# Start, output and routing table of a four-stage transformer kernel: first batch taken alone, output rows written by the last five tiles, last product in halves, table of tiles on GpSimd

## The reference

```python
x = x + xattn0(layernorm(x), ctx, Wq, Wkv, Wout)          # 16 heads of 16, softmax
x = x + ffn0(layernorm(x), ...)                           # 704 hidden, fake-quantised to 8 bits, silu(gate) * up
x = x + xattn1(layernorm(x), ctx, ctx, gates...)          # 4 heads of 64, mLSTM decay, RMS norm
x = x + ffn1(layernorm(x), gate_w, w1, w3, w2)            # 8 experts of 1024, the best 2 of each token
# ffn1: probs = softmax(x @ gate_w); top 2, weights normalised to sum 1;
#       sum over the two experts of weight * ((silu(x @ w1) * (x @ w3)) @ w2)
```

## Time and profile before

| what | value |
|---|---|
| time, median of 3 runs | 757.08 us (752.0 to 757.09) |
| time of the profiled execution | 756.54 us |
| its span | 754.8 us |
| busy: TensorE, VectorE, ScalarE, GpSimd | 657.7, 500.0, 375.3, 291.9 us |
| chain that ended last, by engine | TensorE 58%, VectorE 20%, issue 8%, ScalarE 5%, DMA 2% |
| mean granted clock of TensorE | 0.952 of 2.4 GHz |

### The profile page before, as it was taken

The page is one execution under the profiler, slowest core; times in us unless marked ns, Lnnn a source line. Parts: engine busy times, 40 slices in busy tenths (PEclk is TensorE's granted clock), DMA queues, the critical chain, the costliest instruction groups (busy, mean ns, idle before and its releaser), DMA issues.

```text
span 754.8 us, 17035 instructions
## 1 busy us (share of the span) xinstructions
PE 657.7 (87%) x4890; PEld 464.8 (62%) x4890; DVE 500.0 (66%) x1180; ACT 375.3 (50%) x878; POOL 291.9 (39%) x358
## 2 busy tenths in 40 slices
PE   2799999997777776898099999999999999999992
PEld 2588888886534545786056666666666666666661
DVE  6389899998588967797954746555464747554430
ACT  1366666665686643786223535363543635543320
POOL 3111111121153625577233736464553637543321
PEclk9799999999999999699589999999999999999996
DMA  8200000000300005336405253533415264421114
GB/s 282 47 15 14 14 14 14 14 0 1 112 0 1 0 1 172 128 82 226 135 23 174 49 150 76 150 85 84 140 31 153 73 181 126 116 43 29 31 15 125
DMA packets 47414, 59.01 MB, mean 78 GB/s; under 512 B 13328, under 2 KB 41168, under 8 KB 47056
## 3 DMA queue, kind: packets, MB, share of 16 engines
q1 hardware_dynamic: 39808, 47.72, 19.5%
q0 software_dynamic: 7536, 10.44, 7.8%
HBM read 145.96 MB, written 11.73 MB: 209 GB/s over the span
## 4 chain that ended last, share of the span: by engine, by line
PE 58%; DVE 20%; issue 8%; ACT 5%; DMA 2%; POOL 2%; DVEq 2%; ACTq 1%; SPq 0%; POOLq 0%
PE psum L1052 19%; PE psum L1074 11%; PE psum L752 5%; PE psum L1065 4%; PE psum L736 3%; PE psum L759 3%; PE psum L772 2%; ACT region L1346 2%; PE psum L791 1%; PE psum L741 1%; PE psum L714 1%; DVE region L1759 1%; DVE region L1777 1%; PE psum L779 1%; DVE region L1956 1%
## 5 line engine op out<-in xcount | busy, mean ns | idle before, releaser
L1052 PE MATMUL psum<-region 128*128 (+1 forms) x936 | 214.8, 379 | 1.6 <-DVE region L1952 1.6
L1052 PEld LDWEIGHTS psum<-region 128*128 128x128 bf16 x936 | 91.5, 98 | 95.5 <-DVE region L1952 1.2
L1329 ACT ACTIVATE region<-psum 128x512 f32<-128x512 f32 x78 | 46.5, 597 | 179.6 <-PE psum L1052 178.7
L675 POOL DMA_INDIRECT sum_dram<-region,row_token x39 | 75.2, 1927 | 135.3 <-DVE region L1948 135.3
L1074 PE MATMUL psum<-region 128*128 (+1 forms) x936 | 110.5, 275 | 5.3 <-DVE region L1956 5.3
L1074 PEld LDWEIGHTS psum<-region 128*128 128x128 bf16 x936 | 91.4, 99 | 18.9 <-issue 7.5
L1931 DVE TENSOR_TENSOR region<-psum,region 128x512 f32<-128x512 f32 x78 | 53.8, 690 | 68.3 <-ACT region L1329 68.3
L545 POOL TENSOR_TENSOR region<-region,pair_mask 128x256 f32<-128x256 f32 x32 | 21.3, 687 | 128.3 <-ACT region L1114 128.3
L1956 DVE TENSOR_TENSOR region<-psum,region 128x1024 bf16<-128x1024 f32 x39 | 47.6, 1221 | 17.7 <-ACT region L1337 17.5
L667 POOL DMA_INDIRECT region<-xrow_dram,row_token x39 | 41.4, 1062 | 38.0 <-DVE row_token L1917 13.6
L1421 DVE TENSOR_REDUCE region<-psum 128x8 f32<-128x1024 f32 x32 | 39.0, 1218 | 18.4 <-PE psum L752 18.4
(11 more groups left out here) (298 smaller groups left out, 1220.3 us busy)
## 6 DMA issues: line engine op xcount, KB each, us to landing
region<-in_L_ffn_w SPq DMA_DIRECT2D x117, 1024.0 KB
region<-in_ctx SPq DMA_DIRECT2D x32, 128.0 KB, 2.4
xrow_dram<-region SPq DMA_DIRECT2D x1, 2080.0 KB, 7.8
x_sb<-in_x SPq DMA_DIRECT2D x4, 512.0 KB, 8.0
region<-in_ctx SPq DMA_DIRECT2D x2, 1024.0 KB, 7.0
region<-neg_max_dram SPq DMA_DIRECT2D x1, 2048.0 KB, 11.5
sum_dram<-x_sb SPq DMA_DIRECT2D x1, 2048.0 KB, 7.5
region<-neg_max_dram SPq DMA_DIRECT2D x4, 256.0 KB, 4.0
```

The lines of the kernel that those rows point to most:

```text
L675: pool.indirect_dma_start(sum_dram, bass.IndirectOffsetOnAxis(ap=row_token[:, t:t + 1], axis=0), y_d[:, t % 2, :], None, compute_op=ALU.ad ...
L1052: last = mm(psum[:, 2 * f + n, :], (xT_lo if xl else xT_hi)[:, p, k, :], weights_at(place, wl, n, k * F1 + f * FH, FH), start=(i == 0), st ...
L1329: act_fn(sil_d[:, f, :], psum[:, 2 * f, :], ACT.Silu).then_inc(sil_d_ready, 1)
```

## The change

1. **Start.** SyncE loads batch 0 of x alone, then context 0, Wq, Wkv, batches 1 to 3, context 1, batches 4 to 7, Wout, batches 8 to 15. VectorE makes the statistics of batch 0, norms it, goes on with batches 1 to 3, norms batch 1, then batches 4 to 7; batches 8 to 11 and 12 to 15 are made inside steps 0 and 1. GpSimd's powers are in five lots (`X_LOTS`), the last three behind the masks of batches 0, 1 and 3. The products wait for Wq and Wkv only. TensorE gets 14, 2 and 6 fillers ahead of the transposes, the products and the scores of batch 0.
2. **Table of tiles.** The lines 1858 to 1874 leave VectorE. GpSimd computes the same table in 27 instructions, from `eend`, ahead of its first gather. VectorE waits for `info_ready` 2, which GpSimd gives behind that gather, ahead of its first low half of the weights, and takes x's low part ahead of the second. TensorE's 40 fillers become 20.
3. **Weight loads.** SyncE's loop over the tiles is written out, and each tile's expert and flag are read once instead of three times.
4. **Output.** After 34 of the 39 additions (`DIRECT`) SyncE copies `sum_dram` to the output. For each of the last five tiles GpSimd gathers the sums of its rows (`gather_sums`, the first from `sum_dram`, the others from the output), VectorE adds them to the weighted product, and GpSimd writes the rows to the output (`write_rows`). The gather waits until the write of the tile before has landed, the writes wait for SyncE's copy.
5. **Last product.** The 16 matmuls with the high part of h of the last tile come first, behind five fillers, without a wait for the low part; the 8 with the low part follow.

```diff
@@ start, SyncE
-            sp.dma_start(x_sb[:, 0:4, :], x_v[:, 0:4, :]).then_inc(x_loaded[0], 16)
+            sp.dma_start(x_sb[:, 0:1, :], x_v[:, 0:1, :]).then_inc(x_loaded[0], 16)
+            sp.dma_start(ctx_sb[:, 0, :], ctx_in[0, :, :]).then_inc(ctx_loaded[0], 16)
             sp.dma_start(wq_sb[:], wq.rearrange("(t p) n -> p t n", p=P)).then_inc(w_loaded, 16)
-            sp.dma_start(ctx_sb[:, 0, :], ctx_in[0, :, :]).then_inc(ctx_loaded[0], 16)
             sp.dma_start(wkv_sb[:], wkv.rearrange("(t p) n -> p t n", p=P)).then_inc(w_loaded, 16)
+            sp.dma_start(x_sb[:, 1:4, :], x_v[:, 1:4, :]).then_inc(x_loaded[1], 16)
...
@@ start, GpSimd
+            X_LOTS = (slice(0, 1), slice(1, 4), slice(4, 8), slice(8, 12), slice(12, B))
+            def x_rstd(i):
+                part = X_LOTS[i]
+                pool.wait_ge(ln_chain, 3 * part.stop)
+                nc.gpsimd.tensor_tensor(rstd[:, part], rstd[:, part], minus_half[:, part], ALU.pow).then_inc(rstd1_ready, 1)
...
             for b in range(B):
                 mask_k(b, b % 2)
+                if b in X_RSTD_AT:
+                    x_rstd(X_RSTD_AT.index(b) + 2)
@@ start, TensorE
+            keep_clock(START_CLOCK[0], 7)
             front_transposes(0, 0, 1)
-            pe.wait_ge(w_loaded, 48)
+            keep_clock(START_CLOCK[1], 7)
+            pe.wait_ge(w_loaded, 32)
             front_products(0, 0)
+            keep_clock(START_CLOCK[2], 7)
             step(0, 0, loads=1)
@@ start, VectorE
+            x_stats(0, 1)
+            norm(0, 0)
+            x_stats(1, 4)
+            norm(1, 1)
+            x_stats(4, 8)
...
-            step(0, 0)
+            step(0, 0, late=[lambda: x_stats(8, 12)])
             late = [[] for b in range(B)]
+            late[1] = [lambda: x_stats(12, B)]
@@ table, GpSimd
+            pool.wait_ge(d_chain, ENDS_STEP)
+            for e in range(E):
+                nc.gpsimd.tensor_scalar(ended[:, 0, e, :], iota_t, eend[:, e:e + 1], None, ALU.is_ge)
+            link_p(nc.gpsimd.tensor_scalar(eend2, etiles, 0.5, None, ALU.is_gt))
+            link_p(tt(ended[:, 1, :, :], ended[:, 0, :, :], eend2.unsqueeze(2).to_broadcast([P, E, NT]), ALU.mult))
+            link_p(tt(ended[:, :, 0:4, :], ended[:, :, 0:4, :], ended[:, :, 4:8, :], ALU.add))
+            link_p(tt(ended[:, :, 0:2, :], ended[:, :, 0:2, :], ended[:, :, 2:4, :], ALU.add))
...
+            nc.gpsimd.tensor_scalar(te, te, -1.0, float(E), ALU.mult, ALU.add).then_inc(info_ready, 1)
+
+            pool.wait_ge(chosen_ready, 3)
             pool.wait_ge(rows_stored, 64)
             gather_rows(0)
+            nc.gpsimd.memset(pause_p[:, 0:1], 0.0).then_inc(info_ready, 1)
@@ table, VectorE
-            link_d(tt(tcmp, eend.unsqueeze(1).to_broadcast([P, NT, E]), iota_t.unsqueeze(2).to_broadcast([P, NT, E]), ALU.is_le))
-            link_d(nc.vector.tensor_reduce(te, tcmp, AX.X, ALU.add))
...
+            dve.wait_ge(info_ready, 2)
             first_low(0)
-            first_low(1)
-            info = [None, tile_values(1)]
...
             x_low(0, 0)
+            first_low(1)
+            info = [None, tile_values(1)]
             first_low(2)
@@ output, GpSimd
+            def gather_sums(t):
+                pool.wait_ge(sum_added, 16 * t)
+                pool.wait_ge(y_ready, t)
+                rows = bass.IndirectOffsetOnAxis(ap=row_token[:, t:t + 1], axis=0)
+                if t == DIRECT:
+                    pool.indirect_dma_start(sums_sb[:], None, sum_dram, rows).then_inc(gather_begun, 16)
+                else:
+                    pool.indirect_dma_start(sums_sb[:], None, out_rows, rows, bounds_check=B * P - 1, oob_is_err=False).then_inc(gather_begun, 16)
+            def write_rows(t):
+                pool.wait_ge(y_ready, t + 1)
+                pool.wait_ge(out_stored, 16)
+                pool.indirect_dma_start(out_rows, bass.IndirectOffsetOnAxis(ap=row_token[:, t:t + 1], axis=0),
+                                        y_d[:, t % 2, :], None, bounds_check=B * P - 1, oob_is_err=False).then_inc(sum_added, 16)
...
-            for t in range(NT - 3, NT):
-                add_rows(t)
+            for t in range(NT - 3, NT):
+                write_rows(t)
+                if t + 1 < NT:
+                    gather_sums(t + 1)
@@ output, SyncE and VectorE
+            sp.wait_ge(sum_added, 16 * DIRECT)
+            sp.dma_start(out_rows, sum_dram[0:B * P, :]).then_inc(out_stored, 16)
+            sp.wait_ge(out_stored, 16)
             sp.wait_ge(sum_added, 16 * NT)
-            sp.dma_start(out.rearrange("b p d -> (b p) d"), sum_dram[0:B * P, :]).then_inc(out_stored, 16)
...
+                    dve.wait_ge(gather_begun, 16 * (t - DIRECT) + 32)
+                    nc.vector.scalar_tensor_tensor(out=y_d[:, p, :], in0=psum[:, 7, 0:D], scalar=w_col[:, bass.ds(t, 1)],
+                                                   in1=sums_sb[:], op0=ALU.mult, op1=ALU.add).then_inc(y_ready, 1)
@@ last product, TensorE
-            down_d(NT - 1, places[NT - 1])
+            keep_clock(LAST_CLOCK, 6)
+            pe.wait_ge(hT_high, NT)
...
+            pe.wait_ge(hT_low, NT)
+            for f in range(F1 // P):
+                last = mm(psum[:, 7, 0:D], hT_lo[:, f, :], weights_at(place, 0, 2, f * D, D), start=False, stop=(f == F1 // P - 1))
```

166 lines of the change are left out of this document (94 added, 72 removed).

## The result

The changed kernel ran at 762.63 us median in its first four runs (759.18 to 763.67), the kernel before at 756.99 beside it: a ratio of 1.0079, 95% interval 1.0047 to 1.011. A second series (ten runs) gave 760.56, ratio 1.0067 [1.0044, 1.009]. So the change costs 4 to 6 us, 0.5 to 0.8%: less than the 1% that the forecast named as telling. The forecast was 751.5 in a range of 744.5 to 758; the result lies outside it, on the side of the slower rivals, but by neither of their mechanisms.

The account below looks back on a forecast made before the run. The prediction took TensorE to bound the long middle, leaving start, routing and end to the change: 756.54 + 2.5 (start) + 2.0 (table) - 9.5 (output and last product) = 751.5 us, range 744.5 to 758.

Parts of the forecast that it names:

- Step 1: Start: earlier scores gain only 1.4 us, batch 2's context stays late, TensorE idles and then runs cold: +2.5 us.
- Rival 2: Start: the idle gap does not cost TensorE's clock, -3.9 us, giving 747.6; chance 0.10.
- rival 3: Start: SyncE's queue drains earlier, the context arrives in time and the start pays in full, 738 us; chance 0.06.
- Step 2: Routing: GpSimd's table, delayed by VectorE, is ready at 379.5 and the weights' low halves end later: +2.0 us.
- Rival 1: Routing: VectorE's one-hots do not hold GpSimd, the table keeps up, 746.5 us; chance 0.20.
- Step 3: SyncE's weight loads written out, table values read once: loads are wanted many tiles later, so nothing gained or lost.
- Step 4: Output: copy after the 34th addition hidden, last five tiles write directly; end at 745.3 against 754.8, -9.5 us.
- step 5: Last product by halves: ends between 739.1 and 740.8, before the gather of sums, so worth nothing beyond Step 4.
- G: Output, last five tiles: time of one gather of sums, taken as 2.7 us.
- The end term inside step 4: Program end: 0.5 us taken between the last write's landing and the end, as in the kernel before.
- Rival 4: Output: write and gather round trip becomes the period of the last tiles, 764 to 778 us; chance 0.07.
- Rival 5: Output: the final write is as slow as the copy was, near 7 us, giving 759.5; chance 0.05.

Follow-up runs that it names:

- a: The kernel before with only the change's start (batch 0 loaded and normalised alone, new first-load order, warming matmuls): 757.47 against 756.59 us, ratio 1.0013.
- experiment e: The kernel before with the change's start, plus the third and fourth contexts loaded ahead of the bias loads: 745.49 against 756.36 us, ratio 0.9846.
- f: The kernel before with GpSimd's table of tiles, VectorE made to stand still until the table is done: one run of 763.61 us.
- c: The kernel before with only the change's output: copy after 34 additions, direct writes, last product by halves, SyncE's list written out: 754.04 against 756.59 us, ratio 0.9982.
- d: The changed kernel with the copy and its wait moved ahead of the last weight load in SyncE's list: 761.3 against 756.59 us, ratio 1.0063.
- h: The kernel of c, copying only the first eighth of the rows after addition 34 (other rows stored earlier, lacking sums): 750.68 against 756.36 us, ratio 0.9934.
- k: The kernel before with only the last down product in two halves and five warming matmuls: 754.08 against 756.7 us, ratio 0.9973.
- n: The kernel before with the change's start and GpSimd's table together, output and end as before: 762.36 against 756.7 us, ratio 1.0066.
- o: The changed kernel run again without any edit: 760.56 us, ratio 1.0067 to the kernel before.
- g: The kernel before with token sums kept in the output, GpSimd adding there under an index bound, no final copy: 752.89 against 756.36 us, ratio 0.9939.
- i: The kernel before with early-context start, sums kept in the output and last product by halves: 740.63 against 756.7 us, ratio 0.979.

## Why the prediction was wrong, point by point

- **Step 1, start** (forecast +2.5, ends -1.4 and +2.9; measured +0.9 alone, and 0.94 in the trace). The mechanism held: context at 33 us, idle, then a cold clock. Only the cold stretch was shorter than taken, 35.1 to about 41 instead of 7.8 us. One premise was too strong: that 2.46 us of idleness are enough for the low clock. In a the last product stands behind the same wait and takes 2.8 us, not 4.46. Rival 2 (no loss of clock) is out, rival 3 (the start pays in full) too: nothing drained SyncE's queue sooner. What rival 3 priced at 11 us was right as a price; experiment e collects it with two moved loads.
- **Step 2, table** (forecast +2.0; measured +3.1 alone, 2.7 in the traces). Right mechanism, term too small: the table was forecast for 379.5 of before's time and came at 382.31 - 0.94 = 381.4. Of these 1.9 us the tiles feel little: the low halves of the weights were forecast to end at 390.2 and end at 391.74 - 0.94 = 390.8. f divides the miss of the table: undisturbed I had put the table at 7.8 us, and it takes 9.8 (the comparisons 0.36 each instead of 0.2, which alone is 1.3); the delay by VectorE I had put at 379.5 - 373.1 = 6.4 us, and it is 6.2. So it is the price of the small instructions that was off, not the sum of the waiting. That the waiting came out so well is partly luck: the forecast let one small instruction pass at every border of VectorE's seven big ones, but one comparison alone took 2.31 us beside them, and when the last big one ended, at 375.85, all three wide sums had still to run. Rival 1 (the table keeps up) is out.
- **Step 3, SyncE's loads** (forecast 0). As a price of the loads nothing here speaks against this (no run has the change alone); what it missed is what the list does to the copy behind it, next.
- **Step 4, output: the step that failed** (forecast -9.5 with step 5; measured -2.5 alone, with an interval that reaches +1.1). The forecast had the copy issued at 703.6, as soon as the 34th addition has landed, and a weighting of tile 35 that is 1.2 us late. In c the copy went 4.9 us later than that, the weighting of tile 35 was 6.5 us late (723.12 against 716.65 before), and the last transposes came 3.24 us later. Experiment d corrects the obvious reading: an earlier issue does not help, since the copy then delays the gather of sums for tile 34 (8.6 us instead of 2.8). The forecast took G, the time of a gather, from rows that had no copy beside them. Whichever of copy and gather comes first, the chain of addition, copy, write and gather does not fit into two tiles. h shows it with a copy of 3.0 us.
- **The end term inside step 4** (0.5 us behind the last landing). Wrong by 3.2: the 0.5 was read from an end that waits for a copy. With the last write landed at 748.5 in c, GpSimd's drain holds the program until 752.1. The final write also starts 1.76 us after its weighting (744.01 + 0.48 to 746.25), not 0.28; for tiles 35 to 37 it is 0.83 to 0.85, and what holds the last one longer is not shown. Together: the forecast had the last write at 741.7. In c the write of tile 37 starts 3.8 us later than taken (738.83 against 735.04, of which the stall is 3.24), the round trip behind it takes 5.2 us instead of 5.9, and the last write starts 1.5 later behind its weighting: 741.7 + 3.8 - 0.7 + 1.5 = 746.3, and 746.25 is measured. The time W of that write was 2.1 to 2.3 instead of 3.1, the tail 3.7 instead of 0.5. That accounts for 4.5 - 1.0 + 3.2 = 6.7 of the 6.8 us missing between -9.5 and the -2.7 of c's span.
- **Step 5, halves** (nothing beyond step 4). Right here: the gather of sums ends last. By itself the part is worth 2.6 (k).
- **Rival 4** (write and gather become the period) is out: 2.1 to 2.4 us and 2.1 to 2.2 in c, under the values taken. **Rival 5** (a slow final write) is out by the same rows. The slower side came by a mechanism that was no rival: a long transfer put into the middle of a chain of short ones, and a tail uncovered.

Against the whole: forecast 751.5, found about 761. Of the 9.5 us between, 6.8 are step 4, 1.1 the table, -1.6 the start (in its favour); the rest, some 3, lies ahead of the table in the traces of n, o and d, at a lower clock, and its cause stays open.

## What to carry to other kernels

When a stage starts sooner, look in the queue of its loads for what must now be issued sooner, and count the transfers ahead of it that nobody waits for: moving two contexts ahead of 32 bias loads (0.35 us each) and nine others was worth 11 us here. Before a final transfer is moved out of the way, look at what ends right under it on the other engines; that is the new floor. And a bulk copy does not only take its own time: here the small gathers that started beside it landed with it. So either it must go, or two round trips must fit around it.

## What the runs showed of the hardware

- GpSimd's drain at the program's end: 8.3 us when its last DMA adds, 5.9 when it writes, counted from its own start, 0.2 to 0.3 us ahead of that DMA's row (adding: before, g, i, k; writing: changed kernel, c, d, h). It begins before the data have landed and, where no copy follows, ends 3.3 to 5.4 us after SyncE has seen them.
- An indirect DMA with a bound on its index begins 0.8 us after its release instead of 0.3: in g the last weighting ends at 741.84 and the addition starts at 742.62; before it was 742.55 and 742.83.
- A gather of 128 rows that started 0.25 us after a 2 MB copy landed with the copy, after 8.6 us instead of 2.8 (d against c). The next gather, of tile rows, started 1.6 us after the copy and took 7.6, where 2.9 is the median. The copy moved its 2.10 MB in 48 packets, GpSimd's DMAs in that time 0.35 MB in 193; whether small packets wait behind the large ones is not shown.
- GpSimd and VectorE hold each other up in small operations, too: a flag over 8 columns took 1.11 us beside VectorE's one-hots and 0.23 alone, the whole table 16.0 and 9.8. VectorE's operations on 32 columns took 0.34 and 0.18 us.
